# A decoder layer on one core: selected rows by indexed DMA, the third stage's scores in one step on four strips, a new order, and 72 matmuls of ones

## The reference

```python
# 1 (stage a): causal linear attention, 16 heads of 16
x = x + attn(layernorm(x))
# 2 (stage b): divergence attention against ctx, then a GELU MLP of 1024
x = x + xattn(layernorm(x), ctx, ctx)
# 3 (stage c): 128 of the 256 tokens are routed through a small block
h = layernorm(x)
scores = h @ w_router
_, idx = jax.lax.top_k(scores, 128)
x_sel = jnp.take_along_axis(h, idx[:, :, None], axis=1)
att = softmax(causal(q @ k.T / 4))           # of rmsnorm(x_sel, g1), order = rank
x_attn = (att @ v) @ W_out.T
h2 = rmsnorm(x_sel + x_attn, g2)
x_ff = (silu(h2 @ W1.T) * (h2 @ W2.T)) @ W3.T
out = h.at[idx].set(x_sel + x_attn + x_ff)
x = x + out
```

## Time and profile before

| | |
|---|---|
| median of three runs | 951.96 us (951.67 to 952.5) |
| the profiled execution: span | 947.8 us |
| TensorE matmuls busy | 883.4 us (93%), 7652 instructions |
| VectorE busy | 727.6 us (77%) |
| ScalarE busy | 595.2 us (63%) |
| GpSimd busy | 218.6 us (23%) |
| granted TensorE clock | full in nearly all 40 slices |
| DMA | 25.05 MB, 26 GB/s on average |

### The profile page before, as it was taken

The page is one execution under the profiler, slowest core; times in us unless marked ns, Lnnn a source line. Parts: engine busy times, 40 slices in busy tenths (PEclk is TensorE's granted clock), DMA queues, the critical chain, the costliest instruction groups (busy, mean ns, idle before and its releaser), DMA issues.

```text
span 947.8 us, 21833 instructions
## 1 busy us (share of the span) xinstructions
PE 883.4 (93%) x7652; PEld 750.3 (79%) x7652; DVE 727.6 (77%) x1670; ACT 595.2 (63%) x1582; POOL 218.6 (23%) x379
## 2 busy tenths in 40 slices
PE   7888999999999999999999999999999999998987
PEld 4657797978879797887979788787979788786855
DVE  4878878787887878888787879788787878866342
ACT  4365757667574767657575766757576675745533
POOL 0215122121313122221312222231321222121100
PEclk9999999999999999999999999999999999999999
DMA  7220100101010100101010010101000010000000
GB/s 261 68 82 2 35 1 13 35 12 33 11 33 0 37 7 11 33 11 33 0 44 0 11 33 11 33 11 33 0 17 28 11 33 22 12 2 11 2 13 12
DMA packets 20465, 25.05 MB, mean 26 GB/s; under 512 B 1488, under 2 KB 18000, under 8 KB 20432
## 3 DMA queue, kind: packets, MB, share of 16 engines
q1 hardware_dynamic: 18992, 20.33, 6.6%
q10 hardware_dynamic: 1440, 4.28, 1.4%
HBM read 20.41 MB, written 4.19 MB: 26 GB/s over the span
## 4 chain that ended last, share of the span: by engine, by line
PE 64%; DVE 20%; ACT 7%; issue 7%; DMA 1%; POOL 0%; DVEq 0%; SPq 0%; ACTq 0%; POOLq 0%
PE bank L1064 21%; PE bank L1370 4%; PE bank L1166 4%; PE bank L1356 4%; PE bank L1331 3%; PE bank L1245 3%; PE bank L1253 3%; PE bank L1424 2%; DVE before L950 2%; ACT L615 2%; PE bank L1319 2%; PE bank L1184 2%; PE bank L1457 2%; PE bank L1080 2%; DVE prob L850 2%
## 5 line engine op out<-in xcount | busy, mean ns | idle before, releaser
L652 ACT ACTIVATE w_raw_or_stage_c<-bank,c_nmax 128x128 f32<-128x128 f32 x256 | 90.6, 375 | 12.3 <-DVE c_nmax L981 12.3
L615 ACT ACTIVATE prob<-bank,b_folded 128x256 f32<-128x256 f32 x128 | 53.7, 471 | 46.0 <-PE bank L1064 45.8
L981 DVE TENSOR_REDUCE c_nmax<-bank 128x4 f32<-128x512 f32 x64 | 43.5, 683 | 48.1 <-PE bank L1356 48.1
L809 DVE TENSOR_TENSOR a_s<-bank,const 128x512 f32<-128x512 f32 x112 | 71.8, 677 | 9.0 <-PE bank L1166 6.4
L729 DVE TENSOR_TENSOR b_s_lo<-prob,b_s_hi 128x512 fp32r<-128x512 f32 x64 | 54.2, 848 | 27.3 <-ACT b_s_hi L503 27.3
L426 POOL TENSOR_TENSOR a_tr_lo<-a_norm,a_tr_hi 128x512 fp32r<-128x512 f32 x16 | 21.0, 1310 | 216.9 <-ACT a_tr_hi L503 216.9
L402 POOL TENSOR_TENSOR x<-x,vectors_by_row 128x512 f32<-128x512 f32 x16 | 20.7, 1292 | 161.7 <-DVE w_raw_or_stage_c L975 161.7
L652 ACT ACTIVATION_READ_ACCUMULATOR w_raw_or_stage_c<-bank,c_nmax 128x1 f32 x256 | 55.1, 215 | 0.0
L799 DVE RECIPROCAL a_e<-a_e 128x512 f32<-128x512 f32 x16 | 53.4, 3340 | 0.0
L1064 PE MATMUL bank<-b_s_hi,w_mlp_hi 128*128 128x256 f32 x256 | 44.8, 298 | 4.8 <-ACT prob L615 4.6
L1475 PE MATMUL bank<-ones_bf 128*128 128x512 bf16 x164 | 46.7, 410 | 1.0 <-POOL ones_bf L400 1.0
(11 more groups left out here) (257 smaller groups left out, 2818.4 us busy)
## 6 DMA issues: line engine op xcount, KB each, us to landing
x_in<-in_x SPq DMA_DIRECT2D x16, 256.0 KB, 2.7
qc<-in_ctx SPq DMA_DIRECT2D x16, 256.0 KB, 3.2
b_f<-in_ctx_t SPq DMA_DIRECT2D x16, 256.0 KB, 3.4
out<-w_raw_or_stage_c SPq DMA_DIRECT2D x16, 256.0 KB, 2.1
w_raw_or_stage_c<-in_w ACTq DMA_DIRECT2D x4, 512.0 KB, 5.4
w_raw_or_stage_c<-in_w_gu ACTq DMA_DIRECT2D x4, 341.0 KB, 3.0
w_raw_or_stage_c<-in_w_a SPq DMA_DIRECT2D x2, 384.0 KB, 4.5
w_raw_or_stage_c<-in_w ACTq DMA_DIRECT2D x2, 384.0 KB, 4.4
```

The costliest lines, as they stand in the source:

```text
L615: act_in(prob[:, 2 * (j % 2) + n, :], b0[:, n * T:(n + 1) * T], ACT.Gelu, bias=b1p[:, f:f + 1]).then_inc(b_gelu.sem, 1)
L652: act_in(c_e[g % 2][:, j * R:(j + 1) * R], (c1, c2)[g % 2][:, j * R:(j + 1) * R], ACT.Exp, bias=c_nmax[:, n:n + 1], accum_out=c_den[:, hea ...
L809: tt(heads(A_MASKED[t][n][:, :]), heads(A_SCORES[n][:, :]), tri.unsqueeze(1).broadcast_to([P, 4, P]), ALU.mult).then_inc(a_scput.sem, 1)
L981: nc.vector.tensor_reduce(c_nmax[:, 4 * g:4 * g + 4], heads((c1, c2)[g % 2][:, :]), axis=AX.X, op=ALU.max, negate=True).then_inc(c_max.sem, 1)
```

## The change

Rows are picked and put back by address. The normed tokens, `x + bias` and each token's scale now stand side by side in one tile (`norm_x2_rms`, 513 columns used). SyncE's `store_rows` writes it to a table in DRAM. The rank is counted by VectorE alone (`c_rank_`, a compare with an accumulated sum, two instructions). `c_sel_` makes one selection matrix in bfloat16, and `c_idx_` (TensorE, two matmuls of one column) turns it into the list of the 128 tokens' numbers. GpSimd's `c_pick_` reads those rows from the table by an indexed DMA into `picked_rows`. `c_hsc_` scales them and `c_ht_` is now two transposes. `c_h2put_` (VectorE) adds the picked rows to the attention's projection. GpSimd's `c_ob_` writes `x + h` for all tokens and SyncE stores it; GpSimd's `c_hx_` adds up the residual, `c_y_` the final result, and GpSimd's `c_put_` writes the 128 rows over the output by a second indexed DMA, once the store has landed. `c_rank_` and `c_scat_` of TensorE, `c_before_`, `c_selu_`, `c_ylo_` and `c_done_` of VectorE and `c_yhi_` of ScalarE are gone.

The scores of all 16 heads are one step, `c_score_`, on four strips and four banks (c0, c1, c2, a2), and stage a's `a_k_` waits for the bank that it now shares. ScalarE loads the set of functions that holds both exp and ln ahead of `a_qout_`.

`ORDER` is new and its deepest step now stands four rounds back, so 20 rounds are written instead of 19. `WARM_AT` holds 72 matmuls of ones: 48 in rounds 0 to 3 and 24 in rounds 16 to 18 (before: 65 in rounds 0 to 2 and 85 in rounds 16 to 18). SyncE's loop now issues the next ctx, the table's rows, the store, the next transposed ctx, the next x.

```diff
-a_y+ c_w2 c_att+ b_up_1+ b_down_0+ b_up_2+ c_dput+ b_gelu_1+ a_yhi+ b_ghi_1+ a_mean c_o+ b_glo_1+ c_w3 c_w0
...
+c_w2 a_kput+ c_ff_0++ c_ff_1++ c_gtlo_1++ c_rstd+ c_ht+ a_score_0+ b_fput+ b_fmean+ b_htp+ a_sput+ c_hsc+
+b_sexp+ c_gthi_0++ b_fnormed+ c_gthi_1++ a_mask+ a_mean a_dput+ c_w7 a_scput_0+ b_hlo+ a_scput_1+ c_qk+
...
+WARM_AT = {(0, 'a_q'): 2, (0, 'a_ktp'): 3, (0, 'a_state'): 1, (1, 'a_score_0'): 2, (1, 'a_score_1'): 5, (1, 'a_att_0'): 1, (1, 'a_proj'): 7, (1, 'a_tp'): 1, (1, 'a_q'): 1, (1, 'b_dtp'): 1, (1, 'b_rtp'): 2, (2, 'a_score_0'): 2, (2, 'b_htp'): 1, (2, 'b_up_0'): 2, (2, 'a_att_0'): 1, (2, 'b_up_3'): 1, (2, 'b_v'): 1, (2, 'a_q'): 1, (2, 'c_sbc'): 1, (2, 'c_idx'): 9, (3, 'c_ht'): 3, (16, 'c_idx'): 3, (16, 'b_fd'): 3, (17, 'b_htp'): 2, (17, 'b_up_1'): 2, (17, 'c_etp_0'): 1, (17, 'c_etp_2'): 2, (17, 'c_etp_3'): 1, (18, 'c_ht'): 1, (18, 'c_score'): 1, (18, 'c_etp_0'): 4, (18, 'c_etp_1'): 1, (18, 'c_etp_2'): 2, (18, 'c_etp_3'): 1}
...
-        x2 = sb("x2", [P, TT, D])
+        rows = sb("norm_x2_rms", [P, TT, 2 * D + 4])
+        c_norm, x2 = rows[:, :, 0:D], rows[:, :, D:2 * D]
...
+        picked = sb("picked_rows", [P, 2 * D + 4])
+        x_sel, x2_sel, r1_sel = picked[:, 0:D], picked[:, D:2 * D], picked[:, 2 * D:W]
...
+        C_SCORES, EXP_T = (c0, c1, c2, a2), (c0, c1, c0, c2)
+        EXP_T_FREE = (4, 8, 12, 16)
...
+            def store_rows(b):
+                sp.wait_ge(*c_normed(b))
+                sp.sem_inc(passed.sem, 1)
+                sp.wait_ge(*c_rms1(b))
+                sp.sem_inc(passed.sem, 1)
+                if not first(b):
+                    sp.wait_ge(*picked_in(b - 1))
+                    sp.sem_inc(passed.sem, 1)
+                sp.dma_start(token_rows_by_p, rows[:, :, 0:W]).then_inc(rows_out.sem, 16)
...
+            with sp.Fori(2, B - 1) as i:
+                next_ctx(i - 1)
+                store_rows(i - 2)
+                store(i - 2)
+                next_ctx_t(i - 1)
                 next_x(i)
...
+                    pool.wait_ge(*rows_out(b - 1))
...
+            def c_ob_(b):
+                pool.wait_ge(*c_normed(b))
+                if not first(b):
+                    pool.wait_ge(*out_done(b - 1))
+                nc.gpsimd.tensor_tensor(ob[:, :, :], x2, c_norm, ALU.add).then_inc(c_ob.sem, 1)
+
+            def c_pick_(b):
+                pool.wait_ge(*c_idxput(b))
+                pool.wait_ge(*rows_out(b))
+                if not first(b):
+                    pool.wait_ge(*c_hx_s(b - 1))
+                    pool.wait_ge(*c_h2put(b - 1))
+                pool.sem_inc(passed.sem, 1)
+                nc.gpsimd.indirect_dma_start(
+                    picked[:, 0:W], None, token_rows[:, :], bass.IndirectOffsetOnAxis(ap=index[:, 0:1], axis=0)) \
+                    .then_inc(picked_in.sem, 16)
+
+            def c_hx_(b):
+                pool.wait_ge(*c_h2put(b))
+                pool.wait_ge(*picked_in(b))
+                if not first(b):
+                    pool.wait_ge(*c_y(b - 1))
+                nc.gpsimd.tensor_tensor(c_hx, c_h2[:, :], x2_sel, ALU.add).then_inc(c_hx_s.sem, 1)
+
+            def c_put_(b):
+                pool.wait_ge(*c_y(b))
+                pool.wait_ge(*c_kept(b))
+                pool.wait_ge(*out_done(b))
+                pool.sem_inc(passed.sem, 1)
+                nc.gpsimd.indirect_dma_start(
+                    out[:, :], bass.IndirectOffsetOnAxis(ap=index_out[:, 0:1], axis=0), y_out, None) \
+                    .then_inc(y_stored.sem, 16)
...
+                nc.scalar.preload_act_table_set("natural_log_exp_and_others")
...
+            def c_h2sq_(b):
+                act_e.wait_ge(*c_h2put(b))
+                act_in(flat(c_hT[:, :, :]), c_h2[:, :], ACT.Square, scale=1.0 / D ** 0.5, accum_out=c_sq2[:, :]) \
+                    .then_inc(c_h2sq.sem, 1)
...
+            def c_rank_(b):
                 dve.wait_ge(*c_sbc(b))
+                for t in range(TT):
+                    if t:
+                        dve.wait_ge(*c_rank(b, t))
+                    stt(tie[:, :], b0[:, 0:T], c_sc[:, t:t + 1], tie_bound[:, t, :], ALU.subtract, ALU.is_gt,
+                        accum_out=c_rk[:, t:t + 1]).then_inc(c_rank.sem, 1)
...
+                    ts(sel[:, t, :], iota_bf[:, :], c_rk[:, t:t + 1], None, ALU.is_equal).then_inc(c_sel.sem, 1)
...
+            def c_idxput_(b):
+                dve.wait_ge(*c_idx(b))
+                if not first(b):
+                    dve.wait_ge(*picked_in(b - 1))
+                nc.vector.tensor_copy(index[:, :], b0[:, T:T + 1]).then_inc(c_idxput.sem, 1)
+
+            def c_hsc_(b):
+                dve.wait_ge(*picked_in(b))
+                ts(c_h[:, :], x_sel, r1_sel, None, ALU.mult).then_inc(c_hsc.sem, 1)
...
+            def c_h2put_(b):
+                dve.wait_ge(*c_xo(b))
+                tt(c_h2[:, :], c2[:, 0:D], x_sel, ALU.add).then_inc(c_h2put.sem, 1)
...
+                dve.wait_ge(*c_hx_s(b))
+                if not first(b):
+                    dve.wait_ge(*y_stored(b - 1))
+                tt(y_out, c1[:, 0:D], c_hx, ALU.add).then_inc(c_y.sem, 1)
...
+            def c_idx_(b):
+                pe.wait_ge(*c_sel(b))
+                for t in range(TT):
+                    last = mm(b0[:, T:T + 1], sel[:, t, :], token_bf[:, t:t + 1], start=t == 0, stop=t == TT - 1)
+                last.then_inc(c_idx.sem, 1)
...
-            def c_ht_(b):
-                pe.wait_ge(*c_sels(b))
                 for c in range(DC):
-                    for t in range(TT):
-                        last = mm(c0[:, c * R:(c + 1) * R], c_norm[:, t, c * P:(c + 1) * P], sel_s[:, t, :],
-                                  start=t == 0, stop=t == TT - 1)
+                    last = nc.tensor.transpose(c0[:, c * R:(c + 1) * R], c_h[:, c * P:(c + 1) * P], ident)
                 last.then_inc(c_ht.sem, 1)
 
...
-            def c_score_(p):
-                def step(b):
-                    if p == 0:
-                        pe.wait_ge(*c_qkput(b))
-                        pe.wait_ge(*c_selu(b))
-                    else:
-                        pe.wait_ge(*c_exp(b, 8))
-                    for bk in (c1, c2):
-                        mm(heads(bk[:, :]), ident_bf[:, :], mask_bf[:, :].unsqueeze(1).broadcast_to([P, 4, P]),
-                           start=True, stop=False, skip_group_check=True)
-                    for c in range(DC):
-                        for n, bk in ((2 * p, c1), (2 * p + 1, c2)):
-                            r = 32 * n
-                            last = mm(bk[:, 2 * c * R:2 * (c + 1) * R], cq[r:r + 32, c, :],
-                                      ck[r:r + 32, c, :, :].rearrange("p m k -> p (m k)"), start=False, stop=True,
-                                      skip_group_check=True)
-                    last.then_inc(c_score.sem, 1)
-                return step
+            def c_score_(b):
+                pe.wait_ge(*c_qkput(b))
+                pe.wait_ge(*c_vput(b))
+                if not first(b):
+                    pe.wait_ge(*c_y(b - 1))
+                if not at_least(b, B - 2):
+                    pe.wait_ge(*a_scput(b + 2, 7))
+                for bk in C_SCORES:
+                    mm(heads(bk[:, :]), ident_bf[:, :], mask_bf[:, :].unsqueeze(1).broadcast_to([P, 4, P]),
+                       start=True, stop=False, skip_group_check=True)
+                for c in range(DC):
+                    for n, bk in enumerate(C_SCORES):
+                        r = 32 * n
+                        last = mm(bk[:, 2 * c * R:2 * (c + 1) * R], cq[r:r + 32, c, :],
+                                  ck[r:r + 32, c, :, :].rearrange("p m k -> p (m k)"), start=False, stop=True,
+                                  skip_group_check=True)
+                last.then_inc(c_score.sem, 1)
...
-                for t in range(TT):
-                    mm(c2[:, 0:D], sel[:, t, :], c_norm[:, t, :], start=t == 0, stop=False, skip_group_check=True)
...
```

## The result

| | before | after |
|---|---|---|
| median of the runs | 952.23 us (951.67 to 953.55) | 921.10 us (919.85 to 923.12) |
| ratio, 95% interval | | 0.968 (0.966 to 0.970) |
| profiled execution | 947.8 us | 918.0 us |
| a round | 54.39 us | 51.64 us |

The kernel is faster, by 31 us where 60 were forecast, and 29.5 us slower than the forecast of 891.6. That 921 us lie inside is luck. The page of the kernel after begins with busy time, share of the span and instructions of each engine, then come the granted clock in 40 slices and two lines on the DMAs that are new (KB where the page knows them, median us to landing).

What follows compares the result with a forecast made beforehand. TensorE was taken to bound the loop: a round of 54.4 - 4.2 + 0.5 = 50.7 us, 13 rounds saving 48.1 and the ends 12.3, so 947.8 became 887.4 of span, 891.6 us with 4.2 around it; range 866 to 930 us.

Steps and rivals of the forecast that it cites:

- What bounds the kernel: In the loop TensorE idles only 2.5 us a round; work taken from its queue comes off the round.
- TensorE's work: Per round: gathers, scatter, rank, narrower c_ht_ and four-strip scores, less c_idx_, save 4.2 us.
- VectorE stays near 42 us: VectorE's busy time in a round of 50 us, after compares and sums go and others come in.
- rival 4: Indexed DMA starves in GpSimd's queue while VectorE is busy: round 57.6 us, time 981 us, slower; chance 8%.
- Waits: New waits in a round: 0.5 us for the exponentials, 0 for the pick, 0 for the load of x.
- rival 1: ScalarE's sixteen heads of exponentials leave TensorE waiting 3 us a round: 53.2 us, time 924 us; chance 15%.
- The pick: Indexed DMA behind c_idx_: 2.7 us or twice that, hidden under a cover of 10.0 us, cost taken as 0.
- rival 2: x comes late, VectorE waits 1.5 us in a_mean_: round 52.2 us, time 911 us; chance 10%.
- The end: Last two rows: the last gets 5.3 us shorter, the row before it 3 us.
- The lead-in: Stretch up to the first row's end: saves between 0 and 8.4 us, taken as 4.
- The 78 matmuls of ones that go filled waiting time only: Dropped filler matmuls cost nothing in the sum; a clock falling for want of them would cost a few us.
- A row's way through it is as long: New order one round deeper, yet 4 rounds less a third against 3 and a third; nothing added.

Runs made afterwards that it cites:

- e12_two_halves: Changed kernel with stage c's scores in two halves, masks and products of strips 0 and 1, then of strips 2 and 3: 939.41 us, ratio 0.987.
- e6_gpsimd_order: Changed kernel with GpSimd's b_qb_, c_hx_, c_ob_ and a_kept_ moved to other places of its queue: 912.62 us, ratio 0.959.
- e7_small_sums: Changed kernel with four GpSimd sums (b_qb_, b_kept_, c_ob_, c_hx_) cut to 16 columns of each half from row 1 on: 898.09 us, ratio 0.944.

## Why the forecast was off by 30 us

The forecast's span was 887.4, the measured one 918.0. Of the 30.6 us, 13 x (51.64 - 50.7) = 12.2 lie in the rounds and 18.3 at the ends (246.7 us outside the rounds, forecast 240.7 - 12.3 = 228.4). Of the prediction's own signs of being wrong one came true, "the lead-in grows", and the round of 51.64 us with 3.5 us idle missed its 50 to 51 with 2 to 3. Two steps failed, the work of VectorE and the lead-in; the mechanism held.

- **What bounds the kernel**: right. Work put back on TensorE came back whole (e12_two_halves, 1.18 us a round for 1.05 forecast and an expected 52.6 to 52.8). TensorE doesn't set the round alone: shorter steps on VectorE (e6_gpsimd_order, e7_small_sums) shortened it too, by way of TensorE's waits.
- **TensorE's work**: 3.65 us instead of 4.2. The scores are as forecast (2.04 against 2.11, where two halves took 3.16). `c_idx_` takes 0.2 us instead of "at most 0.1", and one group of stage b (`w_mlp_hi,b_s_hi`) went from 278 to 291 ns a matmul, 3.3 us in the whole run or 0.2 a round. Why, and where the rest is, no run took apart.
- **"VectorE stays near 42 us"**: this step failed. It was 44.3. The missing 0.94 us of a round are, by the windows, 0.55 of TensorE's work and 0.4 of its waits, and the waits hang on this step: with the small sums they were 2.3 us a round instead of 3.5, and the round 50.41. The steps that went were counted, but not what the steps that stayed lie beside. GpSimd got two sums more and an order in which four wide instructions follow each other, and three of them and a copy hold VectorE up. Made small they give back 1.2 us a round, moved 0.7. The prediction had looked at this very thing in rival 4, and from one side only: "nothing in the trace shows an engine held up by another's access". The 1.37 us of `b_glo_` in the trace of before showed it.
- **Waits**: 0.9 us more instead of 0.5. The exponentials cost about the 0.5 us that were put down for them, but one step further on: their transposes wait 3.5 us in the whole run, while `c_att_` waits 8.4 us for the copies `c_et` (0.9 in the kernel before), 0.5 a round. The 3 us a round of rival 1 are out. Beside it stand waits of `c_idx_`, `b_dtp_`, `a_ktp_`, `b_v_` and `c_xo_`, and the old one of 1.0 us for the gate (`L1444 <- L1009`) is gone. That of `b_dtp_` for `c_idxput_` comes with the change and wasn't priced; it costs nothing by itself, as the two runs without it say.
- **The pick**: right for the loop. Its rows were there 3.7 us after the issue (3.5 to 4.5), inside the bounds of 2.7 and twice that. The prediction's estimate of 2.6 us was too low, and the measurement decides. 4.9 us of delay were still covered. Rival 4 is out. **x late**: 0.1 us a round instead of rival 2's 1.5. **Table loads**: four a round, as said.
- **The end**: from row 15's first normalisation (762.68) to the end 155.3 us, before 164.1 (947.8 - 783.67), so -8.8. That stretch holds the forecast's -8.3 for the last two rows and 1.3 rounds of the loop at -3.7, some -13 together, so about 4 us are missing. Most of them stand behind the last step of VectorE: 918.0 - 911.03 = 7.0 us, where the kernel before had 947.8 - 944.15 = 3.7. With no row behind it, the put by address lies open there, and the prediction had no term for it (start us, us):

```profile
911.03 0.42 DVE L1085 TENSOR_TENSOR w_raw_or_stage_c<-bank,w_raw_or_stage_c 128x256 f32<-128x256 f32 x1 [1.07 <-PE bank L1495]
912.33 1.09 POOL L537 DMA_INDIRECT out<-w_raw_or_stage_c,row_of_slot_out  x1 [7.39 <-DVE w_raw_or_stage_c L1085]
```

- **The lead-in**: this step failed, with -4 forecast and +11.9 measured up to row 3's first normalisation. "The 78 matmuls of ones that go filled waiting time only" had its price beside it, "a few us", and it was left out of the sum. The clock fell, and filling brings 5.4 of the 11.9 back. The order of the weight pieces was not looked at, and it gives 5.2. With both and the rest together row 3 starts at 133.9 to 134.5 us; the last 3 to 4 us against the kernel before stay open. How much counts as lead-in depends on the step that is taken as the mark, since the order within a round is new: by the end of stage a's residual (`x<-x,bank`, 190.61 against 182.33) row 3 is 8.3 us late, not 11.9. Lead-in, twelve rounds and end together are +11.9 - 32.9 - 8.8 = -29.8 us, the whole change of the span.
- "A row's way through it is as long" was wrong in the loop: from first normalisation to last step it was 178.9 us (239.34 to 418.25) and is 188.9 (194.05 to 382.93). The prediction's own depths gave 3.67 x 50.7 = 186 against 3.33 x 54.4 = 181 us, a difference that it put at nothing. What that costs is part of the two figures for the ends.

## What to carry to other kernels

Before you call an engine's time unchanged, look at what each of its instructions will lie beside: a step moved onto a helper engine isn't free because that engine is idle, and a mean over a group (860 ns in the loop of the kernel before for `b_s_lo<-prob`, where its like take 692) can hide one instruction in four that waits. If one wait is removed and the round stays, look for the chain that feeds the next one, and test it by shrinking that chain's work, not the wait. Where a schedule is made anew, walk through the first round too, since tables keyed by step names (weights, fillers) get another meaning.

## What the runs showed of the hardware

- VectorE's instructions over two tensors in SBUF, and some over one, wait for a wide GpSimd instruction to end: 0.69 us became 1.45, 0.68 became 1.24 and 1.15, and 0.17 became 1.00. With an operand in a bank they don't (0.68 us at 416.84, beside the sum from 416.94). It goes the other way too: `c_hx_`, 256 columns, took 1.22 us beside `b_diff_` and 0.87 where it was moved. The Trainium skill (SBUF — State Buffer, "SBUF: two separate sides") states an exclusive lock that whichever engine starts first keeps for a whole instruction; of VectorE it takes in instructions with two SBUF inputs, against a GpSimd instruction that reads SBUF, and those in a 2-port mode. The two-input steps here agree (0.69 to 1.45 us); whether the one-input steps ran in such a mode, no run shows.
- Products on 32-row strips overlap without being issued in turn: order 0, 1, 0, 1, 2, 3, 2, 3 took 1.08 us, as 0, 1, 2, 3, 0, 1, 2, 3 did. With a full-array matmul between the pairs it was 1.06 for each.
- The indexed DMA cost GpSimd 1.30 us for the pick and 1.10 for the put of 128 rows, and they landed 3.7 and 2.5 us after issue. Where the pick stood elsewhere (e6_gpsimd_order) it cost 1.11 us; what made it longer, no run took apart.
- In the kernel after the granted clock stood at 0.50 (1.2 GHz) from 22 to 30 us and from 108 to 112 us; TensorE had waited 1.37 us ahead of `a_ktp_` (20.48 us) and 2.72 ahead of `c_idx_` (107.06). With such gaps filled the mean of the first 150 us was 0.98 to 0.99 instead of 0.91.
